# Routed feed-forward after cross-attention: token rows filed whole in expert order, instead of a slot list and gathers

## The reference, cut to what matters

```python
x = x + attention(layernorm(x), ctx)       # 8 heads, 64 context rows per batch
X = layernorm(x)                           # this is what the experts see
s = sigmoid(X @ gate.T)
_, idx = top_k(s + bias, 4)                # 4 of 32 experts per token
w = s[idx] / sum(s[idx])
pos = running count of each expert's tokens, in token order
valid = pos < 512                          # an expert takes its first 512 tokens only
xe[e, pos] = X[token]                      # 32 x 512 slots, empty slots are zero
ye = (silu(xe @ W1) * (xe @ W3)) @ W2      # per expert, 512 -> 256 -> 512
out = x + sum of w * ye[idx, pos] over the valid choices + shared_ffn(X)
```

## Time and profile before

| what | value |
|---|---|
| time, median of 3 runs | 1747.96 us (1747.13 to 1749.15) |
| the profiled execution | 1748.81 us |
| its span, first to last instruction | 1747.0 us |
| PE busy | 1637.0 us, 94% |
| DVE busy | 1378.4 us, 79% |
| ACT busy | 1066.6 us, 61% |
| POOL busy | 1250.9 us, 72% |
| DMA | 274.40 MB, mean 157 GB/s |
| mean granted TensorE clock | 0.979 |

### The profile page before, as it was taken

The page is one execution under the profiler, slowest core; times in us unless marked ns, Lnnn a source line. Parts: engine busy times, 40 slices in busy tenths (PEclk is TensorE's granted clock), DMA queues, the critical chain, the costliest instruction groups (busy, mean ns, idle before and its releaser), DMA issues.

```text
span 1747.0 us, 31933 instructions
## 1 busy us (share of the span) xinstructions
PE 1637.0 (94%) x9056; PEld 1021.2 (58%) x9056; DVE 1378.4 (79%) x3486; ACT 1066.6 (61%) x2368; POOL 1250.9 (72%) x1104
## 2 busy tenths in 40 slices
PE   5999999999999999999999999999767999999994
PEld 4566656566665656666565666655434555555552
DVE  4768988988898898889889888989745777777773
ACT  4767777776777777677767777776413444444441
POOL 2327777777777777777777777777776778778875
PEclk8999999999999999999999999999979999999997
DMA  7556777667666767667777766778538654487512
GB/s 254 149 127 163 177 174 172 166 177 162 157 170 181 173 167 176 162 152 174 176 167 175 175 163 156 168 196 199 140 122 232 140 124 108 119 209 150 89 17 25
DMA packets 474532, 274.40 MB, mean 157 GB/s; under 512 B 352127, under 2 KB 394881, under 8 KB 474356
## 3 DMA queue, kind: packets, MB, share of 16 engines
q1 hardware_dynamic: 429300, 239.03, 54.2%
q0 software_dynamic: 45056, 33.32, 11.2%
HBM read 135.06 MB, written 110.17 MB: 140 GB/s over the span
## 4 chain that ended last, share of the span: by engine, by line
PE 59%; issue 10%; DVE 8%; DMA 7%; ACT 5%; POOL 5%; SPq 3%; POOLq 0%; ACTq 0%; DVEq 0%
PE O_ps L500 14%; PE S_ps L485 13%; PE G_ps L527 5%; PE U_ps L527 4%; PE GE_ps L1580 3%; PE UE_ps L1580 3%; POOL out L1557 3%; PE YE_ps L1620 3%; PE PREP_ps L566 3%; PE PREP_ps L583 3%; PE G_ps L537 2%; PE U_ps L537 2%; DMA pt_l<-p_l 2%; DMA out<-ye,idx_far 2%; SPq L397 1%
## 5 line engine op out<-in xcount | busy, mean ns | idle before, releaser
L923 POOL DMA_INDIRECT slot_table<-tok_line,slot x480 | 508.2, 1059 | 132.0 <-issue 128.0
L932 POOL TENSOR_TENSOR xt_l<-xt,xt_h 128x512 fp32r<-128x512 f32 x128 | 164.9, 1289 | 161.4 <-ACT xt_h L758 161.4
L799 ACT ACTIVATE prob<-S_ps,rs 128x512 f32<-128x512 f32 x128 | 88.1, 688 | 256.0 <-DVE S_ps L1286 251.7
L485 PE MATMUL S_ps<-a_h,xt_h 128*128 128x512 f32 x512 | 211.4, 413 | 2.7 <-DVE m_l L1259 2.7
L500 PE MATMUL O_ps<-m_h,pt_h 128*128 128x512 f16 x512 | 196.7, 384 | 14.4 <-DMA pt_l<-p_l 14.0
L485 PE MATMUL S_ps<-a_h,xt_l 128*128 128x512 f32 x512 | 200.9, 392 | 0.0
L485 PE MATMUL S_ps<-a_l,xt_h 128*128 128x512 f32 x512 | 200.8, 392 | 0.0
L500 PE MATMUL O_ps<-m_h,pt_l 128*128 128x512 f16 x512 | 195.5, 382 | 0.0
L500 PE MATMUL O_ps<-m_l,pt_h 128*128 128x512 f16 x512 | 195.3, 381 | 0.0
L947 POOL TENSOR_TENSOR prob<-prob,rsum 128x512 f32<-128x512 f32 x128 | 135.5, 1059 | 82.0 <-DVE rsum L1314 75.8
L1557 POOL DMA_INDIRECT out<-ye,idx_far x80 | 125.3, 1567 | 36.1 <-issue 25.0
(11 more groups left out here) (245 smaller groups left out, 4774.2 us busy)
## 6 DMA issues: line engine op xcount, KB each, us to landing
xt<-in_xT SPq DMA_DIRECT2D x128, 256.0 KB
xr<-in_x SPq DMA_DIRECT2D x64, 512.0 KB, 4.0
x2aug<-x SPq DMA_DIRECT2D x128, 256.0 KB
out<-xr SPq DMA_DIRECT2D x64, 512.0 KB, 3.4
up_more<-in_w SPq DMA_DIRECT2D x36, 256.0 KB, 4.0
slot_table<-tok_line,slot POOLq DMA_INDIRECT x512, 2.1
up_w<-in_w SPq DMA_DIRECT2D x28, 256.0 KB, 4.9
down_more<-in_w SPq DMA_DIRECT2D x18, 256.0 KB, 5.5
```

The costliest lines, as they stand in the source:

```text
L485: last = pe.matmul(S_ps[t % 2][:, :], left[:, kc, :], right[:, b % 2, kc, :], start=(m == 0), stop=(m == 3 * KD - 1))
L799: act.activation(prob[:, t % 2, :, :], S_ps[t % 2][:, :].rearrange("p (h j) -> p h j", h=H), ACT.Exp, scale=rs[:, q % 2, 0, t % 2:t % 2 + ...
L923: pool.indirect_dma_start(table, bass.IndirectOffsetOnAxis(ap=slot[:, g % 2, i, q:q + 1], axis=0), tok_line[:, g % 2, i, :], None, bounds_ ...
L932: pool.tensor_tensor(xt_l[:, t % 2, :, :], xt[:, t % 2, :, :], xt_h[:, t % 2, :, :].bitcast(F32), ALU.subtract).then_inc(xt_lo, 1)
```

## The change

1. `x2aug`, `slot_table`, the DRAM lists, the gathers, and the stores of rows and weights (L389, L413) are gone. There is one DRAM array `slot_rows` of 16384 rows of 560 floats (2240 bytes): 512 values, 32 weights, and 16 more, of which one is the token's number.
2. The ring `xr` has rows of 560 floats. The second layernorm now writes in place into `xr`, the weights and the number go beside it, and the filing DMA writes the whole row from there, still four per tile at step 20. The weights are made at step 19 instead of 20.
3. Since the residual needs the row before the layernorm, ScalarE computes it back (`restore`) into a new buffer `done`, from which the output is stored. The factors for it are two more small DVE operations per pair of tiles.
4. The ring place is freed by the filing (`scattered`) instead of the output store.
5. The first 128 slots of every expert are filled with empty rows by 16 DMAs in steps 1 to 16, instead of 9 DMAs in the set-up.
6. After the last rank, TensorE counts all members (`count_all`), and `windows` turns the counts into the first row of each 128-row load, so that no load reaches past the filled slots further than needed; slots already read by an earlier chunk are barred from the scatter.
7. SP loads an expert's rows with four plain DMAs, three with a start read into a register; POOL only scatters. The wait for the scatter's order stays; a load waits for the landed scatter of the expert six before.
8. A small DVE addition per expert (`address`) makes the scatter's token indices.

```diff
-ROW = D + E
+LINE = 16
+ROW = D + E + LINE
+BIAS_AT, TOKEN_AT, SPREAD_AT, MEAN_AT = range(D + E, D + E + 4)
-ROUTE, MEMBERS, SLOTS_AT, WEIGHTS, OUT, W_STORE, TABLE = 17, 18, 19, 20, 20, 21, 20
+ROUTE, MEMBERS, SLOTS_AT, WEIGHTS, OUT, TABLE = 17, 18, 19, 19, 20, 20
...
                 def load_tokens(g, k):
                     r = g % XRING
-                    after(sp, out_stored[r][k], (g // XRING) * 16)
+                    if g >= XRING:
+                        sp.wait_ge(scattered[(g - XRING) % 2][k], ((g - XRING) // 2 + 1) * 128)
...
+                def fill_first(n):
+                    if n == 1:
+                        sp.wait_ge(zero_set, 3)
+                    sp.dma_start(first_lines[:, 2 * n - 2:2 * n, :],
+                                 empty.unsqueeze(1).to_broadcast([P, 2, ROW])).then_inc(fill_stored, 16)
...
                     if t is not None:
-                        store_rows(t)
                         turn_rows(t)
...
+                    for j in range(2):
+                        g = group_at(n, FFN_DOWN + j)
+                        if g is not None:
+                            restore(4 * g + 2 * j)
+                            restore(4 * g + 2 * j + 1)
+
                     g = group_at(n, ROUTE)
...
+                def restore(t):
+                    g, i = t // 4, t % 4
+                    act.wait_ge(kept, (t // 2 + 1) * 2)
+                    act.wait_ge(x2_lo, t + 1)
+                    after(act, out_stored[i // 2], g * 16)
+                    act.activation(done[:, i, :], x_tile(t), ACT.Identity, bias=row_part(t, 1, MEAN_AT),
+                                   scale=row_part(t, 1, SPREAD_AT)).then_inc(restored, 1)
...
                     for q in range(first, end):
                         pool.indirect_dma_start(
-                            table, bass.IndirectOffsetOnAxis(ap=slot[:, g % 2, i, q:q + 1], axis=0),
-                            tok_line[:, g % 2, i, :], None, bounds_check=SLOTS - 1, oob_is_err=False).then_inc(scattered[g % 2], 16)
+                            slot_rows, bass.IndirectOffsetOnAxis(ap=slot[:, g % 2, i, q:q + 1], axis=0),
+                            xr[:, t % (4 * XRING), :], None, bounds_check=SLOTS - 1,
+                            oob_is_err=False).then_inc(scattered[g % 2][i // 2], 16)
...
+                for q in range(TOP):
+                    for g in (BUT_ONE, LAST):
+                        if q == 0:
+                            pool.wait_ge(slots_ready, 2 * g + 2)
+                            pool.wait_ge(w_ready, g + 1)
+                            pool.sem_inc(passed, 1)
+                        file_slot(g, q)
+                experts_gpsimd(pool, [(out_stored[k], GROUPS * 16) for k in range(2)])
...
+                        dve.scalar_tensor_tensor(row_part(2 * later, 2, MEAN_AT), shift2[:, later % 2, :], -(D ** 0.5), ones_f[:, 0:2],
+                                                 ALU.mult, ALU.mult).then_inc(kept, 1)
+                        dve.reciprocal(row_part(2 * later, 2, SPREAD_AT), rs[:, r, 1, :]).then_inc(kept, 1)
...
-                    dve.tensor_copy(tok_line[:, g % 2], tok[:, 4 * g:4 * g + 4].unsqueeze(2).to_broadcast([P, 4, LINE])).then_inc(slots_ready, 1)
+                    dve.tensor_copy(row_part(4 * g, 4, TOKEN_AT), tok[:, 4 * g:4 * g + 4]).then_inc(slots_ready, 1)
...
+    def load_rows(sp, e, window_i):
+        if e >= RING:
+            sp.wait_ge(added, (e - RING + 1) * 64)
+        for c in range(CHUNKS):
+            first = sp.value_load(window_i[0:1, e, c:c + 1], min_val=0, max_val=c * P) if c else 0
+            sp.dma_start(rows[:, e % RING, c, :].bitcast(F32),
+                         rows_src[e][bass.ds(first, P), :]).then_inc(rows_loaded[e % RING], 16)
...
         for q in range(TOP):
             sp.wait_ge(filed[q], 128)
-            to = q + 1 if q < TOP - 1 else NEAR
-            sp.dma_start(idx_near[:, q:to, :, :], table_src[:, q:to, :, :]).then_inc(idx_loaded[q], 16)
+            load_rows(sp, q, window_i)
...
+        def address(e):
+            dve.wait_ge(rows_loaded[e % RING], (e // RING + 1) * 64)
+            if e >= RING:
+                dve.wait_ge(added, (e - RING + 1) * 64)
+            dve.tensor_tensor(token[:, e % RING, :], rows[:, e % RING, :, TOKEN_AT].bitcast(F32), barred[:, e, :],
+                              ALU.add).then_inc(addressed, 1)
```

More of the change, by code:

```diff
@@ L195, in tokens_and_experts @@
         shift2 = sb("shift2", [P, 2, 2], F32)
-        nb2 = sb("nb2", [P, 2, 2], F32)
         guess_bias = sb("guess_bias", [P, 1], F32)
         ones_f = sb("ones_f", [P, P], F32)
[L199 to L202, removed]
+        bounds = sb("bounds", [P, 4], F32)
+        wo_max, bo_max, v_max, bound = (bounds[:, k:k + 1] for k in range(4))
         power = sb("power", [P, 2], F32)
@@ L555, in rank, with count_all @@
                               start=False, stop=True).then_inc(rank_done, 1)
+                def count_all():
+                    pe.matmul(count_ps, ones[:, :], before[:, :], start=True, stop=False)
+                    for i in range(4):
+                        last = pe.matmul(count_ps, ones[:, :], member[:, i, :], start=False, stop=(i == 3))
+                    last.then_inc(all_counted, 1)
                 def kv(n, bp, q):
@@ L898, in _ @@
                 route_exp(LAST)
+                for i in range(4):
+                    restore(4 * BUT_ONE + i)
                 for c in range(2):
@@ L901, in _ @@
                     last_high(LAST, c)
+                for i in range(4):
+                    restore(4 * LAST + i)
                 act.wait_ge(kv_done, PAIRB * 2)
@@ L1383, in _ @@
                 slot_spread(BUT_ONE)
+                for k in range(5):
+                    weigh_ops(BUT_ONE, k)
                 slot_list(BUT_ONE)
@@ L1391, in _ @@
                 last_hidden(BUT_ONE, 1)
-                for k in range(5):
-                    weigh_ops(BUT_ONE, k)
                 last_low(BUT_ONE, 1)
@@ L1431, with experts @@
 WEIGHT_SETS, EARLY_SETS = 10, 4
-NEAR = 12
-GATHER, TURN, UP, DOWN, SCATTER = 0, 1, 2, 3, 5
+TURN, UP, DOWN = 0, 1, 2
 def expert_steps(step):
-    for n in range(E + SCATTER):
+    for n in range(E + DOWN):
         step(lambda lag, n=n: n - lag if 0 <= n - lag < E else None)
-def experts(nc, stack, ident, w1, w3, w2, out, x2aug, table):
+def experts(nc, stack, ident, w1, w3, w2, out, slot_rows):
     def sb(name, shape, dt):
@@ L1539, in gather @@
                 pool.sem_inc(passed, 1)
-            if e >= RING:
-                pool.wait_ge(y_read, (e - RING + 1) * CHUNKS)
-                pool.sem_inc(passed, 1)
-            for c in range(CHUNKS):
-                landed = gathered[r] if e else first_rows[c]
-                pool.indirect_dma_start(
-                    rows[:, r, c, :].bitcast(F32), None, x2aug,
-                    bass.IndirectOffsetOnAxis(ap=index(e, c), axis=0),
-                    bounds_check=(TOKENS if e >= RING else TOKENS + PAD) - 1, oob_is_err=False).then_inc(landed, 16)
-        def scatter(e):
             if e:
@@ L1557, in scatter @@
                 pool.indirect_dma_start(
-                    out, bass.IndirectOffsetOnAxis(ap=index(e, c), axis=0),
+                    out, bass.IndirectOffsetOnAxis(ap=token[:, e % RING, c:c + 1], axis=0),
                     ye[:, e % 4, c, :], None, bounds_check=TOKENS - 1, oob_is_err=False,
                     compute_op=ALU.add).then_inc(added, 16)
-        def step(at):
-            e = at(SCATTER)
-            if e is not None:
-                scatter(e)
-            e = at(GATHER)
-            if e is not None:
-                if e in (2, 3):
-                    file_last(e)
-                gather(e)
-        file_last(0)
-        expert_steps(step)
+        for e in range(E):
+            scatter(e)
     def experts_tensor(pe):
```

252 lines of the change are left out of this document (108 added, 144 removed).

## The result

The changed kernel takes 1757.34 us (1755.12 to 1761.04, 5 runs) where the kernel before takes 1747.96 (1746.32 to 1751.63): a ratio of 1.0057, interval 1.0043 to 1.0071. It is slower by 0.6%. Of all runs in this document one, 1873.11 us of the kernel before with an earlier scatter, fell into a slower state with a granted clock of 0.86, and no ratio counts it. The forecast, 1741, had the wrong sign; 1757 lies inside the range, 10 us under rival C's lower number, 1767, and is of C's kind.

What follows compares the result with a forecast made beforehand. The prediction took PE to bound the token stage; +16 (token loop), +1 (DMA), -13 (transition) and -10.8 (end) sum to -6.8, giving 1741 us. Its range was 1722 to 1773.

Steps and rivals of the forecast that it cites:

- rival C: Token stage: the second loop becomes the bound through ScalarE's restores, from 2.3 us growth per group; 1767 to 1783, chance 0.25.
- The restore: Token loop: four ScalarE restores per four tiles, partly hidden; +0.25 and +1.2 us in the two down-half steps.
- the earlier weights: Token loop: weights made one step earlier on DVE, +0.45 us in the 9.75 interval and -0.45 in the next.
- The step that failed: Token stage: loop growth turned into 2.2 us lost per sixteen tiles, +16 us over some 120 tiles.
- The cover: Token stage: PE's 38.2 us per four tiles less 36.7 for ACT's exponentials, 1.5 us of slack.
- B: Token stage: the restore is hidden entirely, so the +16 is gone; 1725 us, chance 0.20.
- DMA: Token stage: whole-row filings and moved fills of empty rows fit, with bursts; +1 us, bounds -4 to +24.
- D: First tiles: whole-row filings delay the transposes, up to +24 us instead of +1; 1764, chance 0.05.
- Transition: From token stage to experts: plain row loads replace list and gathers, PE's waits for rows shrink; -13 us, bounds -17 to 0.
- E: Transition gives nothing, because of register loads on SP or a wait for the windows; 1754 us, chance 0.08.
- The end: After the last weighting: without gathers on POOL the last scatter comes earlier; -10.8 us, bounds -8 to -11.
- The lock: VectorE and GpSimd lock a shared port pair, so the shorter token-number copy still waits: 0, at best -0.65 us per group.

Runs made afterwards that it cites:

- the run with half of the restores moved: Changed kernel with only the second pair's restores moved ahead of ScalarE's exponential, the first pair's left behind it: 1747.76 us.
- the kernel with early restores: Changed kernel with both restores in each step of the down half moved ahead of ScalarE's exponential: 1727.76 us, ratio to before 0.9883.

## Why the prediction was wrong

**The restore.** Its effect on the loop was forecast step by step and came: 8.98 and 8.91 against 8.9 and 8.9, the fp16 copy's wait on DVE 0.68 as in the earlier trace rows but 1.2 later, two operations in 1.51 against 1.4. The loop grew by 1.9 (36.64 to 38.53), inside +1.4 to +2.1. (The lower number is a slip: 0.25 + 1.2 + 0.2 less 0.65 is 1.0.) The interval of 9.75 grew by 0.37, near the +0.45 for the earlier weights, and no later interval gave it back.

**The step that failed** is the term made of it: "I take 2.2 us lost per sixteen tiles". It is 4.9 per sixteen over tiles 32 to 112. The text had the 2.4 to 3.8 by which the loop exceeds PE's short pair and took some off for "the lag of one step". Nothing came off. The cover itself was misread: 36.7 is the loop at PE's shortest group, 36.39, and the prediction laid it beside PE's mean of 38.2. The slack of PE's long pair is no cover, as the run with half of the restores moved shows: L is 37.6 there, under PE's mean, and 12 us are lost in 80 tiles. By stretches the token stage lost 0.5 us up to tile 10, 6.9 to tile 32, 24.4 to tile 112 and 9.7 behind it; the place of the restores makes 33.0 of the 41.5, since the kernel with early restores ends its token stage at 1292.7. On top comes what the sum had not at all, the clock. After a wait of 2.0 us (the one wait between 540 and 550 us) in the profile after, the granted clock is 0.50, the lower of its two levels, 1.2 GHz instead of 2.4, and matmuls last 0.63 instead of 0.38 and stand 0.43 apart instead of 0.22:

```profile
544.00:546.00 2.00, 2.00 (x6) 0.67 (x5) 1.97 (x4) 0.43 (x1) 1.39 (x3) 0.50 0.99 366
```

```profile
544.79 0.63 PE L484 MATMUL O_ps<-m_h,pt_h 128*128 128x512 f16 x1
545.21 0.63 PE L484 MATMUL O_ps<-m_l,pt_h 128*128 128x512 f16 x1
```

Of 2736 recorded score and mixing matmuls from 110 to 1237 us 28 last 0.55 us or more, against 2 of 2821 with early restores. The clock does not fall after every wait: it fell at four, of 2.8, 2.5, 2.0 and 2.9 us, and not after waits of 2.3 and 2.2 us (343.7 and 820.3 us), nor once between 110 and 1237 us in the run with half of the restores moved, whose longest wait is 2.6. Of the 33.0 us between the two kernels' token ends, 22.6 are waits for the transposed probabilities to 1237 us, 2.7 such waits behind it (4.5 against 1.8), and some 5.9 the slower clock (28 x 0.21, an estimate from the counts above; no run shows it alone). The other 1.8 stay open.

**Rival C** had the mechanism, its bounds and the point from which it decides, "a loop growth of 2.3", with the cover of 1.5 taken from the mean. The growth was 1.9 and the time was lost all the same, because that cover hardly exists. B fell: it was argued from ACT's idle time before the exponential, and this time helps only work put ahead of it.

**DMA.** Forecast +1; the filings cost about 3, what the fills cost is open. The whole-row issue on POOL was forecast 1.03 by the gather and is 1.08, against 1.06 for the 64-byte filing before. The whole-row filings of the last groups landed 2.1, 3.2 and 5.4 us after their issue (least, median, most), where 64-byte lines took 2.1, 2.1 and 3.8. D's +24 did not come.

**Transition.** The four row loads with their register reads took 4.02 us of SP, forecast 4. In the changed kernel the last token work was late enough to cover the loads; with early restores PE waits for them 1.91 us:

```profile
1294.64 0.85 PE L1596 MATMUL TE_ps<-ident_r,rows 128*128 128x128 f32 x8 [1.91 <-DMA rows<-slot_rows]
```

The stretch from the last token matmul to the last weighting gave -19.0, where -15.5 was forecast (-13 with the +2 to 3 of the windows in it). E fell. With early restores it gave -16.2, so some 3 of the 19.0 are there only because the token stage ended late. The rows' waits that went are 16.9 us. With them came less of the slower clock: in the 60 us from the first transpose the granted clock is 0.94 after (1327 to 1387 us) and 0.81 before (1290 to 1350 us). What each gave was not taken apart. The pace of the expert stage stayed at 12.8 us per expert, as forecast.

**The end.** The last scatter against the last weighting gave -9.2, forecast -10.8. The order wait of 2.14 us before the last expert's scatters was not in the sum. But the time from the last scatter's issue to the end, taken as constant, fell from 8.4 to 3.6, see below. These 4.8 us were luck: no term of the sum had them. The sum missed by 15.3 us, from -6.8 to +8.5: 22.0 more lost in the token stage, 3.5 more won in the transition and 3.2 more at the end, so the gains hid a part of the error in the first term.

**The lock.** The copy of the token's number shrank from 64 to 4 columns and takes 0.865 instead of 0.856: the size is not what it pays. This is what the prediction expected by the rule of the Trainium skill, "SBUF — State Buffer", section "SBUF: two separate sides", and the trace agrees; no run takes POOL's work away beside this copy.

## What to carry to other kernels

Before an operation is put into an engine's order, look on which side of it the engine idles. A busy share of 76% says nothing if the idle time comes before an instruction that waits for work queued behind the new one. Moving one block turned a loss of 9.4 us into a gain of 19.4. Compare a second loop with the shortest stretch of the bound engine that it must feed, not with its mean, and look in the trace whether a wait was followed by a slower clock, since then it costs more than its own length.

## What the hardware showed that was not expected

POOL's closing DRAIN, an instruction at the end of its program, lasts longer in the kernels in which POOL issued gathers. The views of its line in the kernel before and after (count, duration ns, start):

```profile
L339 POOLq DRAIN  x1: 12055/12055/12055, 1734.7 to 1734.7; - x1
```

```profile
L339 POOLq DRAIN  x1: 7318/7318/7318, 1748.0 to 1748.0; - x1
```

It ends 5.4 us after the last scatter landed before (1741.3), and 0.7 after it in the changed kernel (1754.6). In all profiles the last scatter's issue lies 8.1 to 8.4 us before the end with the 128 gathers (before, and its variants) and 3.6 without them. The kernels with and without gathers differ in more than these, and what the drain waits for was not tried.
